# Norm statistics finished on GpSimd, low halves and router taken from PSUM, chunk 0's norms in setup

## What is computed

```python
# layer 0
h = layernorm(x) * (1 + ca) + sa
x = x + ga * (h + scan_part(h))        # norm, z = xn @ W_in, dt = clip(softplus(z @ W_dt + b))
#   per state s of 16: hs = exp(dt * A) * hs + dt * B[s] * z ;  y += C[s] * hs
#   result (y * silu(xn @ W_gate)) @ W_out
h = layernorm(x) * (1 + cb) + sb
x = x + gb * (gelu(h @ W1[7] + b1) @ W2[7] + b2) * softmax(h @ Wr.T)[7]
# layer 1
h = layernorm(x) * (1 + ca) + sa
x = x + ga * layernorm(h + linear_scan(q, k, v, beta) @ Wo + b_o)
h = layernorm(x) * (1 + cb) + sb
h1 = h + (sigmoid(ln(h) @ Wr) * (ln(h) @ Wv)) @ Wo
bids = confidences(ln(h1)) * shares * difficulty + affinity
# of two relu-square experts and one gated expert the one with the highest bid is added, scaled
x = x + gb * (h1 + chosen_expert(ln(h1)))
```

## Time and profile before

| | us |
|---|---|
| median of 3 runs | 3285.47 |
| lowest, highest | 3280.89, 3286.68 |
| profiled execution, span | 3287.9 |
| its own time beside the span | not listed apart |
| PE busy | 2907.9 (88%) |
| PEld busy | 2380.8 (72%) |
| DVE busy | 2739.3 (83%) |
| ACT busy | 2096.2 (64%) |
| POOL busy | 1925.7 (59%) |

### The profile page before, as it was taken

How to read it: one execution, slowest core, us unless ns; L and a number is a source line. 1 busy time by engine, 2 the same in 40 slices (tenths; PEclk the granted TensorE clock), 3 DMA queues, 4 the chain that set the end, 5 groups by cost and what they waited for, 6 DMA issues and landing times.

```text
span 3287.9 us, 45422 instructions
## 1 busy us (share of the span) xinstructions
PE 2907.9 (88%) x14848; PEld 2380.8 (72%) x14848; DVE 2739.3 (83%) x4612; ACT 2096.2 (64%) x3852; POOL 1925.7 (59%) x1541
## 2 busy tenths in 40 slices
PE   6567698998999899898989989899999989998898
PEld 4455477787877778687777868777777877777676
DVE  3777989797998979799898979889897989989541
ACT  2546476676757677675767767576766767575433
POOL 1766667564766757475675756576575647666110
PEclk8558699999999999999999999999999999999998
DMA  4241123231322323232322323232232323223122
GB/s 130 96 159 39 52 81 111 92 102 64 129 82 91 125 78 100 70 118 85 100 103 81 106 79 125 66 106 92 87 109 86 108 76 121 78 71 120 56 103 76
DMA packets 152778, 308.56 MB, mean 94 GB/s; under 512 B 18368, under 2 KB 96984, under 8 KB 135136
## 3 DMA queue, kind: packets, MB, share of 16 engines
q1 hardware_dynamic: 152000, 302.52, 27.6%
q10 hardware_dynamic: 272, 1.57, 0.1%
q0 software_dynamic: 272, 1.57, 0.1%
HBM read 288.27 MB, written 17.35 MB: 93 GB/s over the span
## 4 chain that ended last, share of the span: by engine, by line
PE 48%; DVE 18%; issue 13%; ACT 12%; POOL 5%; DMA 1%; DVEq 0%; SPq 0%; POOLq 0%; ACTq 0%
PE ps_B L1870 11%; PE ps_B L1765 10%; PE ps_A L1765 8%; DVE hs L1527 8%; PE ps_H L1760 7%; DVE acc L1491 5%; PE ps_H L1778 4%; PE ps_B L1760 3%; POOL bu L1100 3%; PE ps_B L1778 3%; PE ps_B L1917 2%; ACT ps_A L1288 2%; DMA bb<-b_rows 1%; DVE hA L1719 1%; ACT acc L1300 1%
## 5 line engine op out<-in xcount | busy, mean ns | idle before, releaser
L1100 POOL TENSOR_TENSOR bu<-z,bb 128x512 f32<-128x512 f32 x1024 | 1294.2, 1290 | 289.9 <-DVE hs L1527 146.7
L1527 DVE TENSOR_TENSOR_SCAN hs<-ps_A,state,bu 128x512 f32<-128x512 f32 x768 | 976.5, 1276 | 21.7 <-ACT ps_A L1288 11.4
L1288 ACT ACTIVATE ps_A<-dt,a_neg 128x512 f32<-128x512 f32 x1024 | 699.3, 686 | 355.7 <-DVE hs L1527 351.5
L1760 PE MATMUL ps_H<-ident,hs 128*128 128x128 f32 x4096 | 652.6, 294 | 195.3 <-DVE acc L1491 123.1
L1760 PEld LDWEIGHTS ps_H<-ident,hs 128*128 128x128 f32 x4096 | 528.3, 151 | 329.2 <-DVE acc L1491 152.0
L1870 PE MATMUL ps_B<-ws_out,hid 128*128 128x256 f32 x2944 | 699.4, 382 | 15.5 <-ACT hid L1437 6.1
L1491 DVE SCALAR_TENSOR_TENSOR acc<-ps_H,ctok,acc 128x512 f32<-128x512 f32 x960 | 700.2, 731 | 8.0 <-PE ps_H L1760 7.1
L1870 PEld LDWEIGHTS ps_B<-ws_out,hid 128*128 128x128 f32 x2944 | 537.0, 191 | 85.1 <-ACT hid L1437 9.9
L1765 PE MATMUL ps_B<-fh,ws_in 128*128 128x512 f32 x1440 | 537.6, 418 | 10.3 <-DVE bl L1680 4.3
L1527 DVE TENSOR_TENSOR_SCAN hs<-ps_A,bu 128x512 f32<-128x512 f32 x256 | 310.9, 1216 | 32.2 <-ACT ps_A L1288 20.0
L1765 PEld LDWEIGHTS ps_B<-fh,ws_in 128*128 128x128 f32 x1440 | 271.0, 188 | 70.5 <-DVE cb L1664 8.1
(11 more groups left out here) (349 smaller groups left out, 4807.7 us busy)
## 6 DMA issues: line engine op xcount, KB each, us to landing
ws_in<-w_split SPq DMA_DIRECT2D x126, 1024.0 KB, 5.4
bb<-b_rows SPq DMA_DIRECT2D x256, 256.0 KB, 3.9
ws_out<-in_L_ffn_V_rwkv SPq DMA_DIRECT2D x64, 512.0 KB, 5.8
ws_out<-in_L_ffn_W SPq DMA_DIRECT2D x32, 512.0 KB, 6.9
xb<-in_L_attn_x SPq DMA_DIRECT2D x16, 512.0 KB, 5.3
n<-in_L_attn_x SPq DMA_DIRECT2D x16, 512.0 KB, 3.9
w_split<-wsp SPq DMA_DIRECT2D x8, 1024.0 KB, 5.6
out<-xb SPq DMA_DIRECT2D x16, 512.0 KB, 3.2
```

What stands on the lines that cost most here:

```text
L1100: pool.tensor_tensor(bu[:, u % 4, :], z[:, d, :], bb[:, s % 2, :], ALU.mult)\
L1288: act.activation(b.t[:, :], dt[:, d, :], ACT.Exp, scale=a_neg[:, d, s:s + 1])\
L1527: dve.tensor_tensor_scan(hs[:, s % 2, d, :], b.t[:, :], bu[:, k % 4, :], state[:, s, d:d + 1] if i % CPB else 0.0, ALU.mult, ALU.add)\
L1760: return pe.transpose(dst, src, ident[:, :])
```

## The change

Four parts:

1. `stats` on DVE ends with the aggregates. POOL makes nm out of the mean, adds EPS, then takes the power and nb.
2. ACT reads a turned bank twice: once into the high half, once back into the bank in place. DVE subtracts out of the bank and frees it. ff is gone. The router's copy is gone; reduction and subtraction read PSUM and the subtraction frees the bank.
3. The two front norms of chunk 0 stand in the setup block on ACT and POOL. x of chunk 0 is loaded ahead of W_dt; the first three rows of the modulation are stored and loaded by themselves as soon as they are made.
4. All places of `PACE` are new.

```diff
 PACE = {
     "sp": {
...
-        "w_fold": 3, "w_in0": 15, "w_in1": 26, "w_out0": 36, "w_in2": 38, "w_out1": 48, "w_in3": 49, "w_out2":
...
+        "w_fold": 12, "w_in0": 25, "w_in1": 25, "w_out0": 41, "w_in2": 41, "w_out1": 56, "w_in3": 56, "w_out2": 57,
...
+        "w_out7": 98, "w_mods": 107, "x": -344, "mod_s": -27, "x_twice": 3, "bc": 3, "b": 27, "mod_f": 76, "ffn_0":
...
     "act": {
...
-        "kvT0": 188, "kvT1": 188, "q": 189, "j_norm": 203, "xlT0": 206, "xlT1": 206, "xlh0": 207, "xlh1": 216,
...
+        "kvT0": 188, "kvT1": 188, "q": 188, "j_norm": 203, "xlT0": 215, "xlT1": 217, "r0": 230, "r1": 231, "sW0": 234,
...
     "dve": {
-        "w_rows": -27, "w_sums": 8, "w_columns": 90, "xnl0": 1, "xnl1": 3, "clip0": 20, "clip1": 20, "clip2":
...
+        "w_rows": 4, "w_sums": 13, "w_columns": 111, "xnl0": -1, "xnl1": 1, "clip0": 3, "clip1": 3, "clip2": 3,
+        "clip3": 6, "a_stats": 100, "low0": 115, "low1": 115, "router": 115, "prob": 121, "ffn0": 144, "ffn1": 145,
...
     "pe": {
-        "w_turn": -103, "w_rows": -98, "w_prod": 27, "w_columns": 39, "xn0": 4, "xn1": 6, "bc": 11, "dt0": 12,
...
+        "w_turn": 8, "w_rows": 10, "w_prod": 19, "w_columns": 28, "xn0": 1, "xn1": 1, "bc": 2, "dt0": 2, "dt1": 3,
+        "dt2": 3, "dt3": 3, "gate0": 7, "gate1": 7, "gate2": 8, "gate3": 8, "ct": 14, "z0": 14, "z1": 16, "z2": 16,
...
@@ rows of the modulation, in setup (DVE)
+                elif (layer, part) == (0, 0):
+                    dve.tensor_copy(goal, ga).then_inc(u_rows_s, 1)
                 else:
                     step(dve.tensor_copy(goal, ga))
@@ setup block: SP, POOL, ACT
                 for n in range(2):
+                    if n == 1:
+                        sp.dma_start(xb[0][:, :, :], x_v[0:1].rearrange("a p t m -> p (a t) m")).then_inc(s_xin.sem, 16)
                     for at, m, src in pieces[n]:
...
+                front = MOD_PARTS["s"][1] * C
+                sp.wait_ge(u_rows_s, 1)
+                sp.dma_start(mods[:, 0:front], modrow[0][:, 0:front]).then_inc(u_mods, 16)
+                sp.wait_ge(u_mods, 16)
+                load_mod(sp, "s", 0)
                 sp.wait_ge(u_rows, 1)
...
-                pool.wait_ge(u_mm, 3)
-                pool.dma_start(wm[1][:, :, :], kp(w["L1_wmod"])).then_inc(u_wm[1], 16)
+                for name in front_norms_pool(pool, 0):
+                    if name == "h0":
+                        pool.wait_ge(u_mm, 3)
+                        pool.dma_start(wm[1][:, :, :], kp(w["L1_wmod"])).then_inc(u_wm[1], 16)
...
-                act.wait_ge(u_load, n_small)
-                act.activation(a_neg[:, :, :], a_neg[:, :, :], ACT.Exp).then_inc(u_exp, 1)
+                for name in front_norms_act(act, 0):
+                    if name == "sum1":
+                        act.wait_ge(u_load, n_small)
+                        act.activation(a_neg[:, :, :], a_neg[:, :, :], ACT.Exp).then_inc(u_exp, 1)
@@ statistics on POOL
-                def rstd(rs, sig):
+                def rstd(own, rs, mv, sig):
+                    own.step(pool.tensor_scalar(rs[:, :], mv[:, :, 1], 1.0, EPS, ALU.mult, ALU.add))
                     pool.tensor_tensor(rs[:, :], rs[:, :], mhalf[:, :], ALU.pow).then_inc(sig.sem, 1)
...
+                def rstd_and_bias(own, rs, nm, nb, mv, sig):
+                    own.mark(pool.tensor_scalar(nm[:, :], mv[:, :, 0], -1.0, None, ALU.mult))
+                    own.step(pool.tensor_scalar(rs[:, :], mv[:, :, 1], 1.0, EPS, ALU.mult, ALU.add))
+                    own.step(pool.tensor_tensor(rs[:, :], rs[:, :], mhalf[:, :], ALU.pow))
                     pool.tensor_tensor(nb[:, :], nm[:, :], rs[:, :], ALU.mult).then_inc(sig.sem, 1)
@@ statistics on DVE
                     for t in range(NT):
                         ins = dve.bn_aggr(mv[:, t, :], st[:, t, :])
-                    own.step(ins)
-                    if nm is not None:
-                        dve.tensor_scalar(nm[:, :], mv[:, :, 0], -1.0, None, ALU.mult)
-                    dve.tensor_scalar(rs[:, :], mv[:, :, 1], EPS, None, ALU.add).then_inc(sig.sem, 1)
+                    ins.then_inc(sig.sem, 1)
@@ high and low halves of the x stream (those of the f stream are changed alike), ACT and DVE
-                    used(act, j, f"{use}{k}")
-                    act.activation(X.fh[:, k, :], X.ff[:, k, :], ACT.Copy).then_inc(X.x_fh.sem, 1)
+                    b = take(act, j, f"{use}{k}")
+                    act.activation(X.fh[:, k, :], b.t[:, :], ACT.Identity, scale=scale, bias=shift)
+                    act.activation(b.t[:, :], b.t[:, :], ACT.Identity, scale=scale, bias=shift).then_inc(X.x_fh.sem, 1)
...
-                        dve.tensor_tensor(X.fl[:, c, :], X.ff[:, c, :], X.fh[:, c, :].bitcast(F32), ALU.subtract)\
-                           .then_inc(X.x_fl.sem, 1)
+                        b = bank_at(j, f"{('xlT', 'hhT')[k]}{c}")
+                        dve.tensor_tensor(X.fl[:, c, :], b.t[:, :], X.fh[:, c, :].bitcast(F32), ALU.subtract)\
+                           .then_inc(b.free, 1)
@@ router (DVE); ACT's lexp now waits for the bank of routerT to be freed
-                    dve.tensor_copy(lg[:, :, :], b.t[:, 0:NT * 8].rearrange("p (t e) -> p t e", t=NT))\
-                       .then_inc(b.free, 1)
-                    used(dve, j, "routerT")
-                    own_step(dve.tensor_reduce(lg_m[:, :], lg[:, :, :], AX, ALU.max))
-                    dve.tensor_tensor(lg[:, :, :], lg[:, :, :], lg_m[:, :].unsqueeze(2).to_broadcast([P, NT, E_MOE]),
-                                      ALU.subtract).then_inc(f_lsub.sem, 1)
+                    logits = b.t[:, 0:NT * 8].rearrange("p (t e) -> p t e", t=NT)
+                    own_step(dve.tensor_reduce(lg_m[:, :], logits, AX, ALU.max))
+                    dve.tensor_tensor(lg[:, :, :], logits, lg_m[:, :].unsqueeze(2).to_broadcast([P, NT, E_MOE]),
+                                      ALU.subtract).then_inc(b.free, 1)
@@ norms h and i (DVE), ahead of centre
+                    dve.wait_ge(X.x_mv.sem, X.x_mv.at(j, 2))
...
+                    dve.wait_ge(X.x_mv.sem, X.x_mv.at(j, 3))
```

More of the change, by code:

```diff
@@ L326, in build @@
         f1l = sb("f1l", [P, KC, CT], F32R)
-        ff1 = over("ff1", [P, KC, CT], "f1l")
         nF = over("nF", [P, NT, C], "f1h")
@@ new lines, in apply, with front_norms_act @@
+        def apply(act, dst, src, rs, nb, sig):
+            for t in range(NT):
+                ins = act.activation(dst[:, t, :], src[:, t, :], ACT.Identity, scale=rs[:, t:t + 1], bias=nb[:, t:t + 1])
+            ins.then_inc(sig.sem, 1)
+        def front_norms_act(act, i):
+            x = xb[i % NX]
+            for n, (ready, at) in enumerate(((s_xin, 16), (s_h0, 1))):
+                yield f"sum{n}"
+                if n == 0:
+                    since(act, s_xg, i)
+                act.wait_ge(ready.sem, ready.at(i, at))
+                for t in range(NT):
+                    ins = act.activation(n0[:, t, :], x[:, t, :], ACT.Identity, accum_out=sum_s[:, t:t + 1])
+                ins.then_inc(s_sum.sem, 1)
+                yield f"sq{n}"
+                act.wait_ge(s_nm.sem, s_nm.at(i, n + 1))
+                for t in range(NT):
+                    ins = act.activation(n0[:, t, :], x[:, t, :], ACT.Square, bias=nm_s[:, t:t + 1],
+                                         accum_out=sq_s[:, t:t + 1])
+                ins.then_inc(s_sq.sem, 1)
+                yield f"norm{n}"
+                act.wait_ge(s_rs.sem, s_rs.at(i, n + 1))
+                apply(act, (x, n0)[n], x, rs_s, nb_s, (s_norm, s_n)[n])
@@ new lines, in front_norms_pool @@
+        def front_norms_pool(pool, i):
+            own = Own(pool, o_pool_n, i)
+            x = xb[i % NX]
+            for n in range(2):
+                yield f"mean{n}"
+                pool.wait_ge(s_sum.sem, s_sum.at(i, n + 1))
+                pool.tensor_scalar(nm_s[:, :], sum_s[:, :], -1.0 / C, None, ALU.mult).then_inc(s_nm.sem, 1)
+                yield f"rstd{n}"
+                pool.wait_ge(s_sq.sem, s_sq.at(i, n + 1))
+                own.step(pool.tensor_scalar(rs_s[:, :], sq_s[:, :], 1.0 / C, EPS, ALU.mult, ALU.add))
+                own.step(pool.tensor_tensor(rs_s[:, :], rs_s[:, :], mhalf[:, :], ALU.pow))
+                pool.tensor_tensor(nb_s[:, :], nm_s[:, :], rs_s[:, :], ALU.mult).then_inc(s_rs.sem, 1)
+                if n == 0:
+                    yield "h0"
+                    mod_ready(pool, "s", i)
+                    pool.wait_ge(s_norm.sem, s_norm.at(i, 1))
+                    own.step(pool.tensor_tensor(x[:, :, :], x[:, :, :], per_tile(m_row("cA0")), ALU.mult))
+                    pool.tensor_tensor(x[:, :, :], x[:, :, :], per_tile(m_row("sA0")), ALU.add)\
+                        .then_inc(s_h0.sem, 1)
+            own.end()
@@ L1163, in x_stream @@
                     X = lane_of(j)
+                    own = Own(pool, X.x_pow, j)
                     def norm(k):
@@ L1654, in x_stream @@
```

(11 more changed lines are left out.)

176 lines of the change are left out of this document (63 added, 113 removed), and 124 rows, old and new, of the table PACE.

## The result

The changed kernel takes **3296.6 us** in the median of 5 runs (3294.5 to 3299.8), the kernel before 3286.7 beside it (3280.9 to 3287.6): ratio 1.0032, 95% interval 1.0021 to 1.0043, so slower by 10 us. The forecast was 3263, faster by 22, with a range that ended at 3288. Both were wrong.

A forecast was written before the change was run, and what follows sets the result against it. The prediction took VectorE, 97% busy in the scans, as the bound. Statistics -15.0 and the start -7.5, all else 0, summed to -22.5 us, from a median of 3285.5 to 3263, range 3236 to 3288.

The forecast's parts named there:

- Statistics, -15.0: Small steps taken off VectorE in the scans' e and m norms: 10.4 and 4.6 us, together 15.0 us saved.
- nE comes at most some 0.1 us later or earlier: e norm in the scans: GpSimd's negation, add and hand-over replace VectorE's 0.69 us, shifting nE by about 0.1 us.
- the norms of the front: Norms a, h, i, j: worth nothing, covered by VectorE's 14.7 us idle there; without that cover, 1.2 to 2.2 us.
- Low halves, 0: ScalarE's paired PSUM outputs, VectorE's subtractions from PSUM: pair 0.1 us worse, six a chunk, costed at nothing.
- ACT is 94 us busy of 130 in the scans: Cover claimed for ScalarE's slightly longer passes, six a chunk; without room they would cost 0.6 us a chunk.
- The rule of contention that I weighed: VectorE instructions with two SBUF inputs contend with GpSimd's reads, one SBUF input doesn't; router subtraction falls to best case.
- Router, 0: Copy dropped ahead of c1; PE waits 0.2 to 1.0 us longer for the subtraction, covered by idle time: nothing.
- The start, -7.5: Chunk 0's norms in setup: PE's turn 13.8 us earlier, 3.7 to 7.4 returned, gain 7.5 taken.
- now stand amid the projections: Chunk 0: PE's w_turn and w_rows, formerly in waiting time, fall among the projections and give back 3.7 to 7.4 us.
- The merge table, 0 with ends of 3.4 us a chunk: New instruction order: taken as 0, ends being VectorE's 3.4 us idle per scan stretch gained or as much lost.
- Only the start shows: Rival, chance 0.16: PE bounds the scans, VectorE's freed 1.0 us a chunk becomes idle; 3278 us.
- GpSimd becomes late: Rival, chance 0.12: GpSimd's adds delay bu and the scans wait, 3325 us; decided above 1.9 us a chunk.

The follow-up runs named there:

- stats_old_order: Kernel before, old merge table, with the statistics finished on GpSimd in all six norms as the only edit: 3294.6 us (+7.6).
- router_only: Kernel before, old order, with only the router's maximum and subtraction read from PSUM: 3286.4 us (+0.3).
- setup_early_turns: Kernel before with chunk 0's norms in setup and three weight-preparation entries (PE w_turn, w_rows, DVE w_rows) moved behind chunk 0's projections: 3277.9 us (-6.6).

## Why the prediction was wrong, by its own steps

**Statistics, -15.0: measured +7.6 (old order), about 0 in the new one.** The step that failed is "15.0 us off the span, if VectorE stays the bound", read from a 97% busy engine, together with "nE comes at most some 0.1 us later or earlier". The timeline of VectorE in the changed kernel at an e norm, against the earlier trace rows:

```profile
1129.21 0.28 DVE L1474 BATCH_NORM_AGGREGATE mv_x<-st_x 128x2 f32<-128x6 f32 x3
1129.41 1.25 DVE L1531 TENSOR_TENSOR_SCAN hs<-ps_A,state,bu 128x512 f32<-128x512 f32 x1
```

The timeline of GpSimd beside it:

```profile
1127.84 2.35 POOL L1230 TENSOR_TENSOR xb<-xb,hA 128x1024 f32<-128x1024 f32 x1 [1.84 <-DVE hA L1740]
1130.15 0.23 POOL L1141 TENSOR_SCALAR nm_x<-mv_x 128x4 f32<-128x4 f32 x1
1130.46 0.19 POOL L1142 TENSOR_SCALAR rs_x<-mv_x 128x4 f32<-128x4 f32 x1
1130.73 1.04 POOL L1143 TENSOR_TENSOR rs_x<-rs_x,mhalf 128x4 f32<-128x4 f32 x1
1131.85 0.20 POOL L1144 TENSOR_TENSOR nb_x<-nm_x,rs_x 128x4 f32<-128x4 f32 x1
```

The scan follows right behind the aggregates, as forecast: VectorE has its 0.69 us. But GpSimd is in an add of 2.35 us when the aggregates end at 1129.49, and begins nm at 1130.15. Before, VectorE's 0.69 us ran beside that add, and the power began 0.2 us behind it; now 0.58 us of small steps stand there, ahead of the power (1130.15 to 1130.73). From the end of the aggregates to nE it is 2.65 us instead of 2.25, in the old order (stats_old_order) as in the new one. PE's wait for nE answers to 6.2 in the earlier trace rows, VectorE's for bu to 3.8 and PE's for acc to 62.8; the changed kernel over ten chunks:

```profile
PE ps_H L1766 <- DVE acc L1495: 50.9, 13, 5.4
PE ps_B L1766 <- ACT nE L727: 18.9, 10, 2.2
...
DVE hs L1531 <- POOL bu L1151: 3.2, 5, 1.4
...
PE ps_B L1771 <- DVE lg L1566: 5.1, 10, 0.5
```

PE's wait for acc fell by 1.2 us a chunk and its wait for nE rose by 1.3: the time went from one wait into the next. Part of this is the new order's (without the statistics it has 58.9 and 9.6). In stats_old_order, where nothing else differs, the wait for acc falls by 0.8 us a chunk and that for nE rises by 1.2. In the old order VectorE then waits for ps_A behind nE on ScalarE; timeline of VectorE in stats_old_order:

```profile
952.20 1.22 DVE L1527 TENSOR_TENSOR_SCAN hs<-ps_A,bu 128x512 f32<-128x512 f32 x1 [1.98 <-ACT ps_A L1291]
```

Waits of VectorE for ScalarE's exponentials over ten chunks, before:

```profile
DVE hs L1527 <- ACT ps_A L1288: 7.2, 10, 0.8
```

and in stats_old_order:

```profile
DVE hs L1527 <- ACT ps_A L1291: 22.9, 20, 2.0
```

That is 1.6 us a chunk more, against the 1.0 that the e and m norms free: a loss in place of the gain. In the new order an exponential stands ahead of nE in either case, nE comes 2.65 us behind the aggregates with the statistics and 2.62 without, and neither a gain nor a loss shows.

I had also costed the norms of the front at nothing. With a, h, i and j moved the front is 0.49 us longer and the stretch ahead of it 0.28 shorter, +0.2 in all; ScalarE's wait for the a norm's nb rises from 2.9 to 3.2 us a chunk. Where the a and the e norm end, an engine waits for the result, so their latency counts and not VectorE's busy time.

**Low halves, 0: measured +14 for f, +1.6 for x.** "ACT is 94 us busy of 130 in the scans" is true of the x pairs' stretch and says nothing of the f pair, which stands in the front, ahead of the first dt. The size was nearly right (0.1 us a tile, measured 0.14, and 0.18 of waits for PE behind it); the cover was not there. 0.63 us in 14 chunks are 8.8, under the interval of +10 to +18, and the whole PSUM part is some 0.5 us a chunk longer in the scans too, hardly more than the 0.3 by which untouched kernels differ there; whether that is real, and so what makes the rest of the 14 and of the 17, stays open. VectorE's side was right. Tile fl of the changed kernel, against the earlier trace rows:

```profile
L1599 DVE TENSOR_TENSOR fl<-ps_B,fh x60: 675/682/693, 427.3 to 3121.7; 128x512 fp32r<-128x512 f32 x60
```

Its tile lg, likewise:

```profile
L1566 DVE TENSOR_TENSOR lg<-ps_B,lg_m x16: 191/191/192, 251.0 to 3084.7; 128x32 f32<-128x32 f32 x16
```

The maxima of 1158 and 1172 ns are gone, the medians are 682 instead of 684 and 191 instead of 839. The rule of contention that I weighed (the Trainium skill, SBUF — State Buffer, Who interferes with whom) agrees with these rows. The higher fixed cost of a PSUM source (the Trainium skill, VectorE: DVE Perf Modes, the TRN2 errata) does not show in them.

**Router, 0: measured +0.3.** Right. By itself (router_only) it makes PE wait 1.3 us for the subtraction where it waited 1.07 for the copy, 0.2 longer, the low end of what I gave, and nothing shows of it; in the changed kernel that wait is 0.5, which the other parts and the order do. What I didn't see is that the Exp takes up what VectorE wins.

**The start, -7.5: held.** Turn at 52.91 us (forecast 52.8), first z at 85.81 (87). By itself, with the three places of the weight preparation moved, this part measures -6.6; from the turn to the first z it takes 33.9 us instead of 28.0, so 5.9 come back, within the 3.7 to 7.4 forecast. Without the three places the part is worth nothing; I had taken them as given ("now stand amid the projections") and not said that the gain hangs on them. The yT of chunk 0 is 13.6 us early in the changed kernel and 9.1 in setup_early_turns (212.2): the other 4.5 are the new order's, inside chunk 0.

**The merge table, 0 with ends of 3.4 us a chunk: this is where the sum could not be made.** The order alone is +62, 4.2 us a chunk and outside my ends; with the edits it is -17. Alone its front is 1.74 us longer and the stretch ahead of it 1.85 shorter; the 4.3 us are in the scans, and with the PSUM part in they are 1.0. Which single place does that stays open: no run takes the table apart, except for the three places at the start.

**The sum as measured**, in the old order: setup +3.3, statistics +7.6, PSUM part +17.4, together +28.3; all edits +27.6. The three parts add within their intervals, so no interplay among them is needed. The fronts say the same: 0.03, 0.49 and 0.65 make 1.17 over before, the kernel with all has +1.12. The new order takes 17 back; of the 18.3 between the two spans, 17 are there by the yT of chunk 1 (384.3 against 401.6), 0.4 a chunk come in the middle (190.45 against 190.88, all of it in the front and the stretch ahead of it, 39.71 against 40.39), and 4 go again in the tail (238.3 us long there). Most of the 17 at the start is the three places: they turn the setup part from +3.3 into -6.6.

**The rivals.** "Only the start shows" had the mechanism: VectorE's freed time became idle. It had the wrong engine, since not PE's continuous rows but the latencies of ScalarE and GpSimd took it, and it didn't see that these could grow. "GpSimd becomes late" didn't happen: VectorE's wait for bu is 0.3 us a chunk, against the 1.9 at which it was to decide. No rival held the edit's own price on ScalarE.

**Two readings of mine were off, and neither enters the sum.** VectorE's busy time in the front is 28.5 us, not 29.0, which is ScalarE's, so its idle time there is 15.2 us. And a, h, i and j have six small instructions, not seven, 1.0 to 2.0 us.

## What to carry to other kernels

An engine that is 97% busy need not be the bound of a stretch in which it waits for other engines' results: follow what releases the first z and the nE, and cost every edit at those places by latency, also on an engine that is 64% busy. Work moved to an idle engine is free only if that engine is idle at that moment; here it stood behind a 2.35 us add. Of a change in four parts, run the parts: here one of them with three places of the order is 7 us faster than before, and the rest costs 17 us on top.

## What the runs showed of the hardware

Two passes of ScalarE out of PSUM, the second back into the same bank, cost no more than other passes out of PSUM: 778 and 750 ns in the median (f1h and ps_B in the changed kernel, against 770 for the scaling before), 0.66 us apart. What they cost by their own length is the 0.14 us per pass by which a copy from SBUF is shorter. And 26 us less of TensorE at 1.2 GHz over the span (2 x 0.004 x 3287) changed the time by nothing that shows (+1.3 us, interval -2 to +4): here the low granted clock stood behind PE's wait, and the wait was for another engine. The chunks' alternation between 188 and 190 us goes on with the shorter low stretches (3.4 and 6.8 us instead of 6.8 and 10.2). Its cause stays open.
